# One table of powers for E and F of a channel in a diagonal state-space layer

## What is computed

```python
dtA = A * dt[:, None]
P = dtA[:, :, None] * jnp.arange(length, dtype=jnp.float32)
Cs = Cc * (jnp.exp(dtA) - 1.0) / A
K = 2.0 * jnp.einsum('hn,hnl->hl', Cs, jnp.exp(P)).real
...
u_m = u * mask[:, None, :]
k_f = jnp.fft.rfft(kernel, n=n)
u_f = jnp.fft.rfft(u_m, n=n)
y = jnp.fft.irfft(u_f * k_f, n=n)[..., :Lq]
y = y + u_m * D[:, None]
return y * mask[:, None, :]
```

## Time and profile before

| | us |
|---|---|
| median of 3 runs | 853.24 (852.15 to 855.84) |
| profiled execution | 853.14 |
| its span, first to last instruction | 851.3 |
| PE busy | 816.7 (96%) |
| PE weight loads busy | 752.9 (88%) |
| DVE busy | 730.0 (86%) |
| ACT busy | 619.2 (73%) |
| POOL busy | 641.3 (75%) |
| transfers, mean | 179 GB/s |

### The profile page before, as it was taken

How to read it: one execution, slowest core, us unless ns; L and a number is a source line. 1 busy time by engine, 2 the same in 40 slices (tenths; PEclk the granted TensorE clock), 3 DMA queues, 4 the chain that set the end, 5 groups by cost and what they waited for, 6 DMA issues and landing times.

```text
span 851.3 us, 22217 instructions
## 1 busy us (share of the span) xinstructions
PE 816.7 (96%) x6168; PEld 752.9 (88%) x6168; DVE 730.0 (86%) x2020; ACT 619.2 (73%) x1717; POOL 641.3 (75%) x708
## 2 busy tenths in 40 slices
PE   0799999999999999999999999999999999999997
PEld 0779998989999999999998999999999999999996
DVE  7878988888888888888888888888888888888886
ACT  4777776777777777777777777777777777777774
POOL 5887776777777878787787878777787877778771
PEclk9999999999999999999999999999999999999999
DMA  5235877777777787777877777777777877777875
GB/s 108 50 74 145 197 189 183 192 186 184 190 187 199 185 193 192 185 197 184 196 185 193 191 186 197 184 195 185 194 191 190 196 184 195 185 194 189 197 191 137
DMA packets 161391, 152.69 MB, mean 179 GB/s; under 512 B 13656, under 2 KB 161240, under 8 KB 161240
## 3 DMA queue, kind: packets, MB, share of 16 engines
q1 hardware_dynamic: 161064, 152.15, 72.5%
q10 hardware_dynamic: 304, 0.26, 0.1%
HBM read 84.02 MB, written 67.30 MB: 178 GB/s over the span
## 4 chain that ended last, share of the span: by engine, by line
PE 89%; DVE 4%; DMA 3%; ACT 1%; SPq 1%; issue 1%; DVEq 0%
PE y L1021 13%; PE y L1023 13%; PE y L1022 13%; PE y L1067 13%; PE v L1038 11%; PE xt_even L1006 6%; PE xt_odd L1006 6%; PE v L1021 3%; PE v L1022 3%; DMA xall<-in_x_dram 3%; PE v L1023 3%; PE y L1016 2%; PE y L1017 2%; SPq L355 1%; ACT room L542 0%
## 5 line engine op out<-in xcount | busy, mean ns | idle before, releaser
L542 ACT ACTIVATE room<-v 64x192 f32<-64x192 f32 (+1 forms) x768 | 235.8, 307 | 171.9 <-DVE v L911 156.0
L911 DVE SCALAR_TENSOR_TENSOR v<-v,RV,mid 128x192 f32<-128x192 f32 (+2 forms) x512 | 192.3, 376 | 55.0
L911 DVE SCALAR_TENSOR_TENSOR mid<-room,RV,v 128x192 f32<-128x192 f32 (+2 forms) x512 | 184.3, 360 | 42.1 <-ACT room L542 23.5
L1021 PE MATMUL y<-thi,uhi 128*128 128x256 f32 x511 | 186.0, 364 | 0.0
L900 DVE COPY_PREDICATED xall<-mask,y 128x512 f32<-128x512 int32 x254 | 174.4, 735 | 1.7 <-issue 1.7
L1021 PE MATMUL y<-fhi,zhi 128*128 128x256 f32 x511 | 154.3, 302 | 1.3 <-DVE zlo L735 1.2
L1023 PE MATMUL y<-thi,ulo 128*128 128x256 f32 x511 | 144.2, 282 | 0.0
L1023 PE MATMUL y<-fhi,zlo 128*128 128x256 f32 x511 | 143.8, 281 | 0.0
L1022 PE MATMUL y<-tlo,uhi 128*128 128x256 f32 x511 | 143.7, 281 | 0.0
L1022 PE MATMUL y<-flo,zhi 128*128 128x256 f32 x511 | 143.7, 281 | 0.0
L521 POOL TENSOR_TENSOR room<-W,B 128x512 f32 (+1 forms) x127 | 141.7, 1116 | 0.0
(11 more groups left out here) (195 smaller groups left out, 1939.6 us busy)
## 6 DMA issues: line engine op xcount, KB each, us to landing
xall<-in_x_dram SPq DMA_DIRECT2D x256, 256.0 KB, 4.6
out_dram<-xall SPq DMA_DIRECT2D x254, 256.0 KB, 3.4
traw<-krows SPq DMA_DIRECT2D x128, 128.0 KB, 3.0
NXY<-B SPq DMA_DIRECT2D x2, 512.0 KB, 6.2
krows<-ksb SPq DMA_DIRECT2D x8, 1.0 KB, 2.2
krows<-ksb SPq DMA_DIRECT2D x8, 4.0 KB, 3.6
krows<-ksb SPq DMA_DIRECT2D x8, 11.0 KB, 4.0
out_dram<-xall SPq DMA_DIRECT2D x1, 128.0 KB, 2.5
```

The lines of the kernel that those rows point to most:

```text
L542: return act.activation(dst, src, ACT.Copy)
L911: return dve.scalar_tensor_tensor(out=out, in0=src, scalar=RV[:, k:k + 1, h], in1=other, op0=ALU.mult, op1=ALU.add)
L1021: pe.matmul(o, a_hi, b_hi, start=start, stop=False, skip_group_check=True)
```

## The change

Only the product of E and F matters for the output, for each mode. Before, all of the factor in front (g, and the l by which X begins) was split as l in E and g in F. Now z, their product for a mode, is split in a complex root and a real rest: with s = |z| and the sign taken so that nothing cancels, the number r = (s + |re z| ± i im z)/2 has r*r = z times a real number. X starts from r, and the same table serves E and F. The real rest is applied to the states: it is computed with the sign as KS, transposed as a new step S, and stored as RV[:, 6]; `z_high` (ACT) multiplies by it in its copy of the states, and `z_low` (DVE) does so before it subtracts. K still uses Y.

- Per channel POOL makes one table of 256 columns (two products, one subtraction) instead of two tables (512 columns). `turn_e` reads it as E and `f_high` and `f_low` read it, mirrored, as F.
- The root is new work in the front: z on POOL (six operations of 64 columns, after level 0 of B), two squares on ACT (after its takes of R), their sum on DVE (n2), a Sqrt on ACT (after its takes of B1, B2 and Y1 at 12), and then a reciprocal and some small operations on DVE.
- DVE makes Y's levels 0 to 2, then the root, then all four levels of X, and then level 3 of Y. POOL no longer doubles a part of X.
- The list STEPS has no Y2 any more, has S as its last step, and another order; there are three banks instead of five. ACT takes every step.
- `turn_x(0, 0)` and its two copies (`x_high`, `x_odd`) move ahead, to behind R on PE (before the 16 warm-up transposes) and behind Sqrt on ACT.
- `first_table` runs once instead of twice. `state_scale` (DVE) is new, and stands between `x_low(0, 0)` and `e_low(0, 0)`.
- b0, which holds B's first rows for `first_table`, is now copied after level 3 of Y is done and after B2 is placed.

The core of the diff:

```diff
-BANKS = 5
+BANKS = 3
...
 STEPS = [("R", 0), ("R", 1),
-         ("B1", 12), ("B2", 12), ("X1", 12), ("X2", 12), ("Y1", 12), ("Y2", 12),
...
+         ("B1", 12), ("B2", 12), ("Y1", 12), ("Y1", 8), ("B1", 8), ("B2", 8),
+         ("X1", 12), ("X2", 12), ("X1", 8), ("X2", 8), ("X1", 0), ("X1", 4), ("X2", 0), ("X2", 4),
+         ("B1", 0), ("B1", 4), ("B2", 0), ("B2", 4), ("Y1", 0), ("Y1", 4), ("S", 0)]
...
             link(level(pool, link, b_table, fine[0], nb_temps, 0))
+            pool.wait_ge(s_yini, 1)
...
+            pool.tensor_tensor(sq_re, y_re, l_re, ALU.mult)
+            pool.tensor_tensor(sq_im, y_im, l_im, ALU.mult)
+            pool.tensor_tensor(u0, y_re, l_im, ALU.mult)
+            link(pool.tensor_tensor(u1, y_im, l_re, ALU.mult))
+            pool.tensor_tensor(z_re, sq_re, sq_im, ALU.subtract)
+            pool.tensor_tensor(z_im, u0, u1, ALU.add).then_inc(s_z, 1)
...
-                pool.tensor_tensor(tw1[:], w1, b1, ALU.mult).then_inc(s_gpa, 1)
-                pool.tensor_tensor(tw2[:], w2, b2, ALU.mult).then_inc(s_gpa, 1)
+                pool.tensor_tensor(tw1, w1, b1, ALU.mult).then_inc(s_gpa, 1)
+                pool.tensor_tensor(tw2, w2, b2, ALU.mult).then_inc(s_gpa, 1)
...
             take(("R", 0), ("R", 1))
...
+            act.wait_ge(s_z, 1)
+            act.activation(sq_re, z_re, ACT.Square)
+            act.activation(sq_im, z_im, ACT.Square).then_inc(s_sq, 1)
             act.wait_ge(s_nb, 1)
             double_b(slice(12, 16))
...
+            take(("B1", 12), ("Y1", 12))
+            act.wait_ge(s_n2, 1)
+            act.activation(m0, n2, ACT.Sqrt).then_inc(s_m0, 1)
+            x_high(0, 0)
+            x_odd(0, 0)
+            take(("Y1", 8), ("Y1", 8))
...
+            act.wait_ge(s_nx, 3)
+            double_x(slice(0, SQ // 2))
+            take(("X1", 0), ("B2", 4))
+            act.wait_ge(s_ny, 3)
+            tables_placed(act, ("B2", 4))
             copy(b0[:, 0], B1[:, 0, :])
             copy(b0[:, 1], B2[:, 0, :]).then_inc(s_b0, 1)
-            take(("X1", 0), ("X1", 4))
+            take(("Y1", 0), ("Y1", 4))
...
-                copy(zhi[j % 2][:, B:], vb[j % 2][:, B:NC * B]).then_inc(s_zhi, 1)
+                act.activation(zhi[j % 2][:, B:], vb[j % 2][:, B:NC * B], ACT.Copy,
+                               scale=RV[:, 6:7, chan(g, j)]).then_inc(s_zhi, 1)
...
-            link(level(dve, link, both, coarse[0], temps, 0))
+            link(level(dve, link, y_table, coarse[0], temps, 0))
             powers(R_POW, NPOW, [(lim, sn), (lre, cs)])
...
+            level(dve, link, y_table, coarse[1], temps, 1).then_inc(s_ny, 1)
+            dve.wait_ge(s_sq, 1)
+            dve.scalar_tensor_tensor(out=n2, in0=sq_re, scalar=1e-30, in1=sq_im, op0=ALU.max, op1=ALU.add).then_inc(s_n2, 1)
+            dve.wait_ge(s_ny, 1)
+            level(dve, link, y_table, coarse[2], temps, 2).then_inc(s_ny, 1)
+
+            dve.tensor_scalar(pos, z_re, 0.0, None, ALU.is_ge)
+            dve.wait_ge(s_m0, 1)
+            link(dve.reciprocal(inv, m0))
+            link(dve.scalar_tensor_tensor(out=inv, in0=n2, scalar=0.25, in1=inv, op0=ALU.mult, op1=ALU.mult))
+            dve.scalar_tensor_tensor(out=u0, in0=m0, scalar=0.25, in1=inv, op0=ALU.mult, op1=ALU.add)
+            link(dve.scalar_tensor_tensor(out=u1, in0=pos, scalar=0.5, in1=z_re, op0=ALU.subtract, op1=ALU.mult))
+            dve.scalar_tensor_tensor(out=NXY[:, SQ - 1, 0, 1, :], in0=pos, scalar=0.5, in1=z_im,
+                                     op0=ALU.subtract, op1=ALU.mult)
+            link(dve.tensor_tensor(NXY[:, SQ - 1, 0, 0, :], u0, u1, ALU.add))
+            link(level(dve, link, x_table, coarse[0], temps, 0))
+            for k in range(1, 4):
+                level(dve, link, x_table, coarse[k], temps, k).then_inc(s_nx, 1)
+                dve.wait_ge(s_nx, k)
+            dve.wait_ge(s_ny, 2)
+            level(dve, link, y_table, coarse[3], temps, 3).then_inc(s_ny, 1)
...
+            def state_scale():
+
+                link(dve.reciprocal(inv, NXY[:, SQ - 1, 0, 0, :]))
+                dve.scalar_tensor_tensor(out=KS[:], in0=pos.unsqueeze(1).broadcast_to([P, 2, N]), scalar=0.5,
+                                         in1=inv.unsqueeze(1).broadcast_to([P, 2, N]),
+                                         op0=ALU.subtract, op1=ALU.mult).then_inc(s_kappa, 1)
...
-                less(zlo[j % 2][:, B:], vb[j % 2][:, B:NC * B], zhi[j % 2][:, B:]).then_inc(s_zlo, 1)
+                dve.scalar_tensor_tensor(out=zlo[j % 2][:, B:], in0=vb[j % 2][:, B:NC * B], scalar=RV[:, 6:7, chan(g, j)],
+                                         in1=zhi[j % 2][:, B:].bitcast(F32), op0=ALU.mult,
+                                         op1=ALU.subtract).then_inc(s_zlo, 1)
...
-            first_table(0)
+            first_table()
             x_low(0, 0)
+            state_scale()
             e_low(0, 0)
-            first_table(1)
...
             turn(("R", 0), ("R", 1))
+            turn_x(0, 0, 0)
+            turn_x(0, 0, 1)
             keep_warm(WARM, pro[BANKS - 1])
             pe.wait_ge(s_bdup, 1)
             turn(("B1", 12), ("B2", 12))
...
+            pe.wait_ge(s_ny, 1)
+            turn(("Y1", 12), ("Y1", 12))
...
+            pe.wait_ge(s_ny, 3)
+            turn(("Y1", 0), ("Y1", 4))
+            tables_placed(pe, ("Y1", 4))
             k_fenced(0)
-            turn_x(0, 0, 0)
-            turn_x(0, 0, 1)
             turn_e(0, 0)
             turn_x(0, 1, 0)
             turn_x(0, 1, 1)
+            pe.wait_ge(s_kappa, 1)
+            turn(("S", 0), ("S", 0))
             chunk_sums(0, 0)
```

More of the change, by code:

```diff
@@ L82, in s4d_kernel @@
         NR = sb("NR", [P, 2, 3, 2, N])
-        sgn = sb("sgn", [P, 2])
+        sgn = sb("sgn", [P, 3])
+        root = sb("root", [P, 10, N])
+        KS = sb("KS", [P, 2, N])
         ksb = sb("ksb", [P, SQ, P])
@@ L150, in s4d_kernel @@
         yb = [[bank(f"y{i}{k}") for k in range(2)] for i in range(2)]
[L152 to L153 removed]
+        pro = [vb[0], vb[1], yb[0][0]]
+        k_banks = [yb[0][1], yb[0][0], yb[1][0], yb[0][0], yb[1][0]]
         b0 = yb[1][1][:, CHUNK:CHUNK + 2 * SQ].rearrange("p (w b) -> p w b", w=2)
         turns = yb[1][1][:, 0:2 * 4 * N].rearrange("p (c k n) -> p c k n", c=2, n=N)
+        z_re, z_im, sq_re, sq_im, n2, m0, inv, pos, u0, u1 = (root[:, i, :] for i in range(10))
         l1r, norm, g_re, g_im, t1, t2, t3 = (small[:, i, :] for i in range(7))
@@ L311, in place, with tables_placed @@
                 return RV[:, i:6:2, :]
+            if name == "S":
+                return RV[:, 6, :]
             if name in ROWS:
                 return {"B1": B1[:], "B2": B2[:], "X1": W1[:, 0], "Y1": W1[:, 1]}[name][:, :, i:i + 4]
-            return W2[:, 1 if name == "Y2" else 0, i:i + 4, :]
+            return W2[:, i:i + 4, :]
         def sign(t):
-            return {("R", 1): sgn[:, 1:2]}.get(STEPS[t], sgn[:, 0:1] if STEPS[t][0] in SIGNED else None)
-        def tables_placed(eng):
-            for t in range(T_K - BANKS, T_K):
+            return {("R", 1): sgn[:, 1:2], ("S", 0): sgn[:, 2:3]}.get(STEPS[t], sgn[:, 0:1] if STEPS[t][0] in SIGNED else None)
+        def tables_placed(eng, last):
+            end = STEPS.index(last) + 1
+            for t in range(end - BANKS, end):
                 eng.wait_ge(s_free[t % BANKS], t // BANKS + 1)
@@ L590, in take @@
                 for t in range(STEPS.index(first), STEPS.index(last) + 1):
-                    if t not in BY_VECTOR:
-                        filled(act, t)
-                        if sign(t) is None:
-                            copy(place(t), four(t)).then_inc(s_free[t % BANKS], 1)
-                        else:
-                            act.activation(place(t), four(t), ACT.Copy, scale=sign(t)).then_inc(s_free[t % BANKS], 1)
+                    filled(act, t)
+                    if sign(t) is None:
+                        copy(place(t), four(t)).then_inc(s_free[t % BANKS], 1)
+                    else:
+                        act.activation(place(t), four(t), ACT.Copy, scale=sign(t)).then_inc(s_free[t % BANKS], 1)
@@ L612, in _ @@
             act.wait_ge(s_nb, 2)
             double_b(slice(8, 12))
-            take(("X2", 12), ("Y2", 12))
-            act.wait_ge(s_nxy, 2)
-            double_xy(slice(8, 12), both)
-            take(("B1", 8), ("Y1", 8))
-            act.wait_ge(s_nxy, 3)
-            double_xy(slice(0, SQ // 2), 1)
-            take(("Y2", 8), ("B1", 4))
-            for t in range(STEPS.index(("B1", 0)), STEPS.index(("B2", 4)) + 1):
-                act.wait_ge(s_free[t % BANKS], t // BANKS + 1)
-            act.wait_ge(s_nxy, 4)
+            take(("B1", 8), ("B2", 8))
@@ L713, in _ @@
             turn_odds(0, 0)
+            take(("S", 0), ("S", 0))
             e_high(0, 1)
@@ L1126, in turn @@
                         pe.wait_ge(s_free[t % BANKS], t // BANKS)
-                    for r in range(3 if STEPS[t][0] == "R" else 4):
```

(1 more changed line is left out.)

132 lines of the change are left out of this document (58 added, 74 removed), and 4 rows, old and new, of the table STEPS.

## The result

The changed kernel takes 868.68 us (median of 4 runs, 864.47 to 869.92) beside 852.99 for the one before: 1.0169 times as long, interval 1.0127 to 1.0211. The forecast was 861.8 with a range of 857.8 to 865.8. The sign was right; the time lies above the range. The profiled execution was the quickest of the four: 864.47, with a span of 862.7.

The account below looks back on a forecast made before the run. PE was taken to bound the loop, so the later front sets the loss: 8.1 - 0.4 + 0.1 + 1.0 = 8.8, with 0.1 rounded off, and 853.14 + 8.7 = 861.8 us; range 857.8 to 865.8.

Parts of the forecast that it names:

- step 4: Front, DVE: reciprocal and five 64-column operations 1.65 us, to 35.3; X done at 43.9, Y's level 3 at 47.75.
- the scale in the loop: z_low +0.07 us on DVE and z_high +0.09 on ACT per channel, covered by PE: worth 0; +0.1 at the end.
- Steps 1 and 2: Front, DVE: Y's levels 0 and 1 done at 24.3; 2.2 us wait for squares, Y's level 2 done at 28.9.
- Step 3: Front, ACT: Sqrt queued behind three takes, magnitude at 33.65; DVE idle since 28.9, a second wait of 4.6 us.
- The rival with the dearer switch: Front, ACT's table switch to Sqrt: held another 1.28 us, all on the chain, 863.1 us in all; chance 0.08.
- Step 5: Front, ACT after X at 43.9: doubling, eight takes, b0, Y1's takes, to 50.35; k_fenced 8.1 us later than before.
- Step 6: From k_fenced to toep: K row through DRAM, same path as before; E and states late by less, 0.4 us given back.
- Step 7: PE's clock in the front: may fall to 1.2 GHz in a gap; ends 0 and +3.1 us, +1.0 taken.
- the forecast's own signs: Front and loop: k_fenced's first matmul at 50 to 53, toep_even at 59 to 62, period still 6.2 us.
- The loop: 128 channels at PE's pace, 6.2 us each; 0.47 us in hand at zlo, 0.16 used: worth 0.
- The rival in which DVE's whole slot becomes the bound: Loop: scale costs 0.30 instead of 0.16, DVE's slot 6.25 us, 0.05 lost per channel, 868 us in all; chance 0.06.
- POOL: Loop: table operations shrink from 512 to 256 columns, at least 1 us less per channel on a covered engine: worth 0.

Follow-up runs that it names:

- PE kept busy: The changed kernel with 110 more unused transposes of the identity on PE, at five places in the front: 865.05 us, 1.0141.
- both kernels with all three: The changed kernel with early Sqrt, root values partly in PSUM and unused transposes: 860.56 us with 110 of these, 859.19 us with 48.

## Where the prediction was wrong, and where it was right

The direction, the order of the waits and their causes came as forecast. The time didn't: one term of the front, the root (step 4), was priced at a third of what it took, and the scale in the loop ("worth 0") wasn't nothing. Errors the other way hid a part of it, and that is luck: the magnitude came earlier and the K path was shorter than forecast.

- **Steps 1 and 2** (Y first, squares): 24.35 measured, 24.3 forecast; the wait 2.25 for 2.2; Y's level 2 done 29.5 for 28.9, as n2 took 0.79, held behind a POOL operation, the same effect as in step 4.
- **Step 3** (a second wait of 4.6, m0 at 33.65): the wait is 3.35 and m0 at 32.96. The order of the queues was right; the 16 warm-up transposes took 2.06 us, not 3.62, as the clock came up at 27.5; the forecast had given this 0.8, it was worth 1.5. The 16 start 1.4 us later than before, which is what the 0.8 stood for; the rest is luck of the execution. The clock comes up anywhere from 27.2 to 30.5 in either kernel, and the same 16 took 2.04 to 3.40 us in the eight profiles with x transposes ahead, 2.62 to 3.62 in the six without. The table load cost its 1.28 and no more: Sqrt started 0.01 us behind it. ACT's operation ahead of the load ended at 31.36, 0.02 us before it. The rival with the dearer switch didn't occur. The Trainium skill, "ScalarE: Activation LUTs", section "What ACT_TABLE_LOAD costs", adds about 1.38 us of drain; the trace shows none on either side of the load, and the measurement decides for this switch.
- **Step 4, the step that failed.** "Five 64-column operations" were priced by size alone: 1.65 with the reciprocal, measured 4.93. All five read both inputs from SBUF and stand beside POOL's operations of 1.26 us; the table steps, which gave the price, read one input from PSUM (the rows name it y, and xt_even in the kernel before). With one input in PSUM the same five took the forecast's price (1.64 with the reciprocal). The levels behind it took what was forecast (X level 3 begins at 42.60, 4.71 after X level 0; forecast 4.75), and so X was done at 46.44 instead of 43.9.
- **Step 5**: from X's end to k_fenced 6.64 for 6.45. k_fenced +10.8 instead of +8.1.
- **Step 6** (the path over K as before): 9.13 us before from k_fenced to toep, 7.83 to 7.94 in the five profiles where the chunk sums were quick and traw in time (PE kept busy, the root in PSUM, without the scale, and both kernels with all three). Before, thi at 50.13 started with no idle time of ACT ahead of it, which speaks for ACT's queue, and not the K row's way through DRAM, as what set it; with the K path later than the rest by more, that queue drops out, which the forecast didn't give back. How much it is, is less sure: four other profiles with the front of before have 8.57 to 8.59, one has 9.12, so it is between 0.6 and 1.3 us, and no experiment took the queue away.
- **Step 7** (clock, +1.0, and the transposes of B1, B2 as the place): the fall in the gap came as said, and its price was 1.1 to 1.3 us behind X, as forecast; but in the first profile the transposes after X ran at the quick pace and the chunk sums at the slow one, in the second the other way round.
- **The sum at the front**: +3.28 (root), -0.69 (m0), +0.19 (step 5), -1.30 (K path), +0.14 (clock, 1.14 for 1.0) is +1.6; toep was forecast at 60.5 and came at 62.05. By the forecast's own signs (k_fenced at 50 to 53, toep at 59 to 62) the first profile is just outside.
- **The loop** ("worth 0, 0.47 us in hand"): the wrong place of the body was read. The nearest place has 0.28, of which 0.15 is hand-over, and the scale uses it up. In the profile of the changed kernel that and the rest behind toep come to 1.15 more than the forecast's -0.4. About 0.5 of it is PE's 0.4 us wait for the first states, which step 6 gave back and which is still there (0.55 at 65.39). The rival in which DVE's whole slot becomes the bound gave 868, close to the median, but it isn't what happened: it takes 6.2 us in the loop, and the channels come every 6.21 us against 6.20, some 1.5 us in all. Its threshold was wrongly drawn too: not the slot's length on the mean decides, but the distance at its tightest place.
- **POOL** worth 0: measured 0.3 us, within -0.6 to 1.2.

1.6 at the front and 1.1 behind it are the 2.7 us between 861.8 and the profiled 864.47. The median lies 4.2 us higher still. The best candidate is the front's own scatter: three profiles have toep at 62.05, 64.52 and, without the scale, 63.21, and the profiled 864.47 was the quickest of its four. The front of before scatters too (toep at 50.08 to 51.64 in six profiles). The means lie 12.2 us apart; with about 1 us in the loop that makes an estimate of 13, where the two measurements of the changed kernel gave 14.4 and 13.4 by their ratios. The other candidate is the loop, which took 799.5 to 804.0 us from toep to the end in the profiles with the changed front. Neither was measured over the timed runs, so this part stays open. Open too is why the tight place costs 0.18 us a body in the kernel before with the scale and 0.06 in the changed one; DVE's slot there is 6.64 us in the one and 6.53 in the other, which says where, not why.

## What to carry to other kernels

A short operation on VectorE with two inputs is priced by what runs on GpSimd at that moment and by where its inputs lie, not by its columns alone: put one input in PSUM, or keep long GpSimd operations away from a dependent chain. Cover in a loop is read at its tightest place, which here is the one behind the branch of an unrolled body, and the hand-over time is taken off before it is called in hand. Where one chain sets the start of the main loop, its delays add: mending the clock, the root and the magnitude moved toep by 1.3, 3.2 and 1.5 us one at a time, and by 6.4 together, with fewer unused transposes; these are single profiles, and two of the unchanged kernel differ by 2.5, so only the sum and the root's share are clear. Work put in to keep an engine busy can itself become the bound: with 110 unused transposes instead of 48 it was 2.9, not 6.4.

## What the runs showed of the hardware

A VectorE operation of 64 columns (fp32, both inputs in SBUF) that takes 0.22 us with GpSimd idle took up to 1.34 beside GpSimd operations of 1.26, and 0.35 beside one of 0.32. Each that was held ended about 0.08 us after a GpSimd operation; one that began just ahead of a GpSimd operation took 0.21. With one input in PSUM, beside the same GpSimd operations, they took 0.21 to 0.23. The Trainium skill, "SBUF — State Buffer", section "SBUF: two separate sides", states it: a DVE operation with two SBUF inputs and a GpSimd operation that reads SBUF exclude each other for the whole instruction, and the one that comes second waits. The runs agree for VectorE's side; whether GpSimd's operation waits no run here shows.

PE's clock rose to 2.4 GHz during nothing but transposes (at 27.5 us; 0.21 us each ahead of it, 0.11 behind) and fell to 1.2 in a gap of 3.98 us (34.3). The rise lies anywhere from 27.2 to 30.5 us in the 14 profiles of this case, though PE's first transposes start at 24.0 to 24.7 in all. In two executions of the same instructions its second low stretch lay at 54.8 to 58.2 and at 48.9 to 52.3. With 110 transposes as filling it stayed at 1.00 from 28 us on.
